# V in two places and other positions for the three steps from values to tokens, in a kernel of deformable convolution and spectral filters on one core

## The reference

```
x = x + silu(batchnorm(deform_conv2d(ln_c(x), offset(x), mask(x), weight)))   # 3x3 taps, bilinear gather of 4 corners per tap
t = tokens(x)                                            # (4, 1024, 64)
t = t + stu(ln_t(t))
# stu: U_plus, U_minus = causal convolutions of u with 16 filters phi (and with signs alternated)
#      out = sum_k s_k U_plus[k] @ Mpp[k] + sum_k s_k U_minus[k] @ Mpm[k] + 3 lags of u @ Mu
#      four branches (whole, half, quarter, eighth of the tokens), mixed by hard/soft weights
x = from_tokens(t)
```

## Time and profile before

| | us |
|---|---|
| median of 3 runs | 757.35 |
| lowest and highest of them | 754.41, 762.09 |
| the profiled execution | 751.24 |
| its span in the trace | 749.4 |

### The profile page before, as it was taken

One profiled execution on the slowest core, in us unless ns is written; L12 is line 12 of the kernel. 1 busy time (PEld: TensorE's weight loads), 2 busy tenths in 40 slices (PEclk: granted clock), 3 DMA queues, 4 the chain that ended last, 5 costly groups with the idle time before them and its releaser, 6 DMA issues.

```text
span 749.4 us, 13126 instructions
## 1 busy us (share of the span) xinstructions
PE 506.5 (68%) x5598; PEld 376.8 (50%) x5598; DVE 314.9 (42%) x800; ACT 179.7 (24%) x421; POOL 292.7 (39%) x295
## 2 busy tenths in 40 slices
PE   5976429246208845785889549891168648999998
PEld 3443105135106613564678329771156327788997
DVE  6467411868602703850438007187009025753000
ACT  1121012113004302321232102240033113334322
POOL 1257750634770372556253732237702745000000
PEclk9966558659557966986999759996569759899999
DMA  8526373811330131222121320113300321000000
GB/s 166 127 79 158 101 204 117 282 56 50 98 105 2 46 107 45 66 71 85 44 64 37 100 64 23 44 44 98 98 21 30 105 64 56 16 2 3 9 2 9
DMA packets 43778, 54.27 MB, mean 72 GB/s; under 512 B 24664, under 2 KB 34142, under 8 KB 43721
## 3 DMA queue, kind: packets, MB, share of 16 engines
q0 software_dynamic: 13824, 37.77, 17.1%
q1 hardware_dynamic: 23841, 13.42, 6.9%
q10 hardware_dynamic: 6056, 2.26, 1.3%
HBM read 50.12 MB, written 3.30 MB: 71 GB/s over the span
## 4 chain that ended last, share of the span: by engine, by line
PE 55%; another core or an unknown queue 25%; issue 10%; DVE 5%; ACT 4%; DMA 1%; SPq 0%; ACTq 0%; DVEq 0%
PE bank L888 30%; PE bank L900 7%; PE bank L760 2%; PE bank L834 2%; PE bank L824 2%; ACT u_conv L661 2%; PE bank L793 2%; PE bank L741 1%; PE bank L795 1%; PE bank L732 1%; PE bank L845 1%; PE bank L919 1%; ACT vT L628 1%; DMA filt<-in_L_ffn_phi_dram 1%
## 5 line engine op out<-in xcount | busy, mean ns | idle before, releaser
L269 POOL DMA_INDIRECT G<-corner_table,idx x288 | 290.0, 1007 | 343.9 <-DVE idx L362 155.2
L888 PE MATMUL bank<-filt,u_hi 128*64 128x256 f16 x2560 | 255.3, 291 | 135.1 <-issue 85.6
L888 PEld LDWEIGHTS bank<-filt,u_hi 128*64 128x64 f16 x2560 | 152.8, 114 | 172.0 <-issue 112.0
L888 PE MATMUL bank<-filt,u_lo 128*64 128x256 f16 x1280 | 198.9, 291 | 15.1 <-issue 15.1
L661 ACT ACTIVATE u_conv<-bank,f_scale 128x256 f32<-128x256 f32 x256 | 118.6, 474 | 303.8 <-PE bank L888 153.6
L900 PE MATMUL bank<-u_conv,mixw 128*64 128x256 f32 (+1 forms) x640 | 94.2, 377 | 9.9 <-issue 9.2
L888 PEld LDWEIGHTS bank<-filt,u_lo 128*64 128x64 f16 x1280 | 84.3, 117 | 24.6 <-issue 22.4
L455 DVE TENSOR_TENSOR G<-G,bank 128x2304 f32<-128x2304 f32 x32 | 81.5, 2548 | 0.3
L467 DVE TENSOR_SCALAR expo<-expo 128x128 f32<-128x128 f32 x16 | 3.6, 227 | 183.1 <-ACT expo L638 172.1
L459 DVE TENSOR_TENSOR V<-G 128x576 f32<-128x576 f32 x32 | 24.3, 758 | 110.0 <-PE bank L825 73.4
L900 PEld LDWEIGHTS bank<-u_conv,mixw 128*64 128x64 f32 x640 | 47.9, 155 | 20.5 <-issue 18.9
(11 more groups left out here) (158 smaller groups left out, 387.3 us busy)
## 6 DMA issues: line engine op xcount, KB each, us to landing
filt<-filter_rows SPq DMA_DIRECT2D x16, 514.0 KB, 9.1
G<-corner_table,idx POOLq DMA_INDIRECT x288
corner_table<-n_uT SPq DMA_DIRECT2D x12, 128.0 KB, 2.9
mixw<-in_x_dram SPq DMA_DIRECT2D x2, 512.0 KB, 6.0
filt<-in_L_ffn_M_phi_plus_dram SPq DMA_DIRECT2D x8, 128.0 KB, 4.9
out_dram<-o_sb ACTq DMA_DIRECT2D x8, 128.0 KB
filt<-n_L_ffn_M_phi_minus_dram ACTq DMA_DIRECT2D x4, 128.0 KB, 4.0
corner_table<-n_uT ACTq DMA_DIRECT2D x4, 128.0 KB, 3.3
```

The lines of the kernel that those rows point to most:

```text
L269: pool.indirect_dma_start(G[:, k, tap, :], None, corners[bp], bass.IndirectOffsetOnAxis(ap=idx[:, q % 2, k, tap:tap + 1], axis=0)).then_in ...
L888: last = pe.matmul(conv_ps[b2][C * src:C * src + C, 0:2 * P].rearrange("c (p a) -> c p a", p=2), u[:, NJ * bp + j2, b2, src], h, start=(j2 ...
```

## The change

V gets a second place, one for each row of a quarter: the even row writes and reads V[:, 0], the odd row V[:, 1]. With that, the write of V for row r waits until row r - 2 has been turned, not row r - 1. To make room, w_diag (used before the passes) and u_conv (used in them) share one tile. And the hosted steps move: of the even row, turning the values from filter 3 to 2, the convolution stays at 4, turning back from 5 to 6; of the odd row, from 11, 12 and 13 to 9, 11 and 13. The programs of VectorE and GpSimd keep their order.

```
-HOSTED_AT = ((3, 4, 5), (11, 12, 13))
+HOSTED_AT = ((2, 4, 6), (9, 11, 13))
...
-        V = sb("V", [P, 2, TAPS * C])
+        V = sb("V", [P, 2, 2, TAPS * C])
...
-        w_diag = sb("w_diag", [P, BRANCHES, 3, P])
...
-        u_conv = sb("u_conv", [P, 2, 2, 2, P])
+        late_tiles = sb("late_tiles", [P, 1536])
+        u_conv = late_tiles[:, 0:1024].rearrange("s (k b p a) -> s k b p a", k=2, b=2, p=2)
+        w_diag = late_tiles[:].rearrange("s (r v d) -> s r v d", r=BRANCHES, v=3)
...
                 if b2 == 0:
-                    dve.wait_ge(val_turned, START + 2 * q + p)
-                dve.tensor_tensor(V[:, b2].rearrange("s (t c) -> s t c", c=C), G[:, k, :, 0:C], G[:, k, :, C:2 * C], ALU.add
+                    dve.wait_ge(val_turned, START + 2 * q + p - 1)
+                dve.tensor_tensor(V[:, p, b2].rearrange("s (t c) -> s t c", c=C), G[:, k, :, 0:C], G[:, k, :, C:2 * C], ALU.add
                                   ).then_inc(v_ready[b2], 1)
...
                     for m in range(4):
-                        pe.transpose(val_ps[b2][:, P * m:P * m + P], V[:, b2, P * m:P * m + P], ident)
-                    last = pe.transpose(tail_ps[0:C, P * b2:P * b2 + P], V[:, b2, 4 * P:4 * P + C], ident)
+                        pe.transpose(val_ps[b2][:, P * m:P * m + P], V[:, r % 2, b2, P * m:P * m + P], ident)
+                    last = pe.transpose(tail_ps[0:C, P * b2:P * b2 + P], V[:, r % 2, b2, 4 * P:4 * P + C], ident)
```

## The result

The changed kernel takes 784.96 us (median of 4, 780.67 to 787.78), the kernel before, run beside it, 755.88 (4 runs, 748.04 to 762.09): a ratio of 1.041, interval 1.034 to 1.048, about 29 to 31 us slower. The profiled execution took 784.31 us against 751.24, 33 us more. The forecast was 773 (758 to 788): the sign and the range hold, the size is half of what came.

A forecast was written before the change was run, and what follows sets the result against it. The time was taken as TensorE's work plus the tails of the runs of gathers. The terms 19.5 + 3.2 + 5 - 11 - 1 = +15.7 us took the median of 757.35 to 773, range 758 to 788.

The forecast's parts named there:

- Part 1: Turn at filter 6, odd row's values at 9: TensorE waits for VectorE's 11.6 us chain in five passes, +19.5 us.
- half is taken back by the nine gathers behind: Lower bound of 15 us on the filter 9 waits: following gathers' tail would absorb half of passes 1 and 5's.
- The clock: Lower granted clock after TensorE's 4.4 us waits in passes 2 and 6: 1.6 us each, +3.2 us.
- my bound of 8: Upper bound of the clock loss, us: all five filter 9 waits put TensorE's array back to half rate.
- Part 2: V once per row: no gain on VectorE, but pass 2's gathers join into one run of 27, +5 us.
- the +5 for the join: Cost in us of pass 2's gathers joining into 27, most matmuls of the former gap moving behind the run.
- Part 3: Runs of 36 gathers in passes 0 and 4 split into 27 + 9, freeing TensorE earlier: -4 and -7, sum -11.
- Part 4: Two filters between hosted steps remove TensorE's waits for the vT copies: -1 us.
- my outer bound: Largest gain allowed for removing TensorE's waits for the vT copies: -2.4 us.
- nothing splits: Rival: the gather runs of passes 0 and 4 stay whole, +30 us, 787; chance 0.18.
- late fetch: Rival: TensorE's slow stretches come from late instruction fetch, not gathers; joining or splitting is irrelevant, +22, 779; chance 0.1.
- the 3.79 us: Pass 2, before: the third set of gathers' wait for V, and V's for turn_values, splitting the run.

The follow-up runs named there:

- run 3: Kernel before with V in two places and only the even row's steps moved, to filters 2, 4, 6: 777.96 us, ratio 1.013.
- run 4: Kernel before with V in two places and only the odd row's steps moved, to filters 9, 11, 13: 787.11 us, ratio 1.028.
- run 6: The changed kernel, unedited, profiled on another chip beside the kernel before: 804.61 us against 770.51, ratio 1.045.
- run 2: Kernel before with only the hosted steps moved (2, 4, 6 and 9, 11, 13), V in one place: 810.02 us, ratio 1.056.
- run 5: The kernel before, unedited, profiled once more on another chip: 767.32 us in its profiled execution.
- run 1: Changed kernel with hosted steps put back at filters 3, 4, 5 and 11, 12, 13, V in two places: 772.55 us, ratio 1.0065 to before.
- run 8: Kernel before with a rest of GpSimd, two small waited-for memsets, after every third gather: 591.41 us, ratio 0.7705.

## Why the prediction was right, and where its sizes were off

**Part 1, TensorE waits for VectorE's chain: right, to a few tenths, in the five passes priced.** Passes 1, 2, 3, 5, 6 were put at 4.8, 4.4, 2.4, 3.5, 4.4 (sum 19.5) and measured 5.06, 4.37, 2.39, 3.90, 4.36 (sum 20.1). Runs 3 and 4 show the rule behind it, filters between exponential and values, at two more distances. Pass 5 scatters more on other chips (4.75 in run 6, 5.59 in run 2). The bound "half is taken back by the nine gathers behind" did not come true: the fourth set waits for the same V, so it moves along with the turn.

**The clock: right in size for pass 6, charged to too few waits.** Windows of the kernel after, TensorE alone, in pass 6, ahead of the turn, behind it, and the next stretch:
```profile
680.00:705.00 25.00, 20.78 (x315) 1.00 0.01 2
705.00:711.00 6.00, 5.86 (x55) 0.72 0.01 3
711.00:716.00 5.00, 5.00 (x90) 1.00 0.00 0
```
0.28 of 6 us are 1.7 us, 1.6 was charged. Waiting 1.95 us (run 4) left that pass at 1.00. In passes 2 and 3, all engines as in the earlier trace rows, the 5 us some 2 us behind the waits of 4.37 and of 2.39 us:
```profile
396.00:401.00 5.00, 5.00 (x65) 4.16 (x66) 2.54 (x3) 2.55 (x6) 4.09 (x4) 0.82 0.31 98
490.00:495.00 5.00, 5.00 (x84) 4.49 (x82) 2.93 (x3) 2.27 (x6) 4.09 (x4) 1.00 0.32 86
```
65 matmuls ran where 84 did. But passes 1 and 5, where I had charged nothing, paid too. The 5 us right behind their waits of 5.06 and 3.90 us, TensorE alone:
```profile
307.80:312.80 5.00, 4.95 (x36) 0.53 0.19 57
646.70:651.70 5.00, 4.93 (x40) 0.66 0.17 52
```
The changed kernel and runs 2 and 6 have 17 waits of 3.9 us and more at filter 9, and behind every one the same 5 us have 0.50 to 0.71, so mostly the 1.2 GHz level. Behind the shorter ones it goes either way: 1.00 behind 2.39 us in the changed kernel and 1.95 in pass 6 of run 4, but in pass 3 of run 6 (2.37 us) and pass 2 of run 4 (1.96 us):
```profile
502.10:507.10 5.00, 4.97 (x48) 0.66 0.19 56
...
397.70:402.70 5.00, 4.94 (x48) 0.66 0.18 56
```
In those 5 us the five waits that I had priced lost 7.4 us (2.35, 1.7, 0, 1.7, 1.65), not 3.2, just under my bound of 8. Passes 1 and 5 came out near their terms all the same, because their granted clock over the whole pass did not change (0.77 and 0.77, 0.74 and 0.75): before, pass 1 had its low stretch at its end instead (0.69 from 313.5 to 320.5). That their totals fit is in part luck.

**Pass 6 adds up, with one term that I had not seen.** 4.36 of waiting, 1.7 of clock, and 1.36 us in which TensorE stood at the start of the pass for u_lo of the odd row. The timeline after:
```profile
664.95 0.23 DVE L468 TENSOR_SCALAR expo<-expo 128x128 f32<-128x128 f32 x1 [13.63 <-ACT expo L639]
...
671.30 0.29 DVE L491 SCALAR_TENSOR_TENSOR u_lo<-u_tok,u_hi 128x128 f16<-128x128 f32 x1
```
The sum is 7.4, as measured. From the exponential (664.6) to u_lo are 6.9 us, and the pass ends 4.4 us behind that exponential. In run 5 it ends 9.1 us behind it, and there is no such wait: TensorE was still held by the nine gathers of pass 5. Windows of run 5, TensorE alone, beside and behind these nine:
```profile
647.00:653.00 6.00, 2.77 (x35) 0.96 0.34 102
653.00:661.00 8.00, 5.59 (x52) 0.60 0.09 29
```
So the last filters cover VectorE's chain only where a tail makes them long. Runs 1, 2, 4 and 6 have the 1.4 us too, run 1 without any step moved, run 3 has not: it goes with where the tail lies, and isn't the moved steps' alone.

**Part 2, the join in pass 2: right in what happened, not shown as its effect.** The waits for V at L459 are gone, and stand at L468, as foreseen. The waits list after (us in total, times, longest):
```profile
DVE expo L468 <- ACT expo L639: 294.0, 14, 43.6
```
That line was 172.1 before; the waits ahead of the write of V, 73.4 behind the turn of V and 35.6 behind "remote", have gone into it, and VectorE is not done sooner. The run of pass 2 is one piece of 27 (337.8 to 372.4) and the pass 14.4 us longer on the first chip. On the second the kernel before had it joined too, at 84.4 us, and the changed one took 92.3, +7.9. The difference between the chips, 6.5 us, is in line with the +5 for the join, but run 1, which has V twice and the run joined, is only 0.65% slower as a whole. So V twice is no sizable loss by itself; the join comes and goes. The term was put on the wrong cause: runs 2 and 5 join with V once. And its price is not shown: in pass 3, 18 + 9 and 27 took the same time (93.5 in run 5, 93.6 before).

**Part 3, the splits: the step that failed.** I had -4 in pass 0 and -7 in pass 4. The splits came as foreseen in both, but brought less, and laid open a wait that I had set to none. Eight profiled executions, with the run of gathers, the wait for V at the odd row's turn and the length of the pass, in us:

| kernel | pass 0: run | wait | length | pass 4: run | wait | length |
|---|---|---|---|---|---|---|
| before | 36 | 0 | 84.5 | 36 | 0 | 73.3 |
| run 5 (before) | 36 | 0 | 84.6 | 27 + 9 | 0 | 69.4 |
| run 1 | 36 | 0 | 86.4 | 36 | 0 | 74.0 |
| run 4 | 36 | 0 | 87.0 | 36 | 0 | 73.6 |
| run 3 | 27 + 9 | 2.8 | 85.5 | 27 + 9 | 3.0 | 72.6 |
| after | 27 + 9 | 6.6 | 89.0 | 27 + 9 | 0.6 | 68.9 |
| run 6 (after) | 27 + 9 | 6.7 | 90.9 | 27 + 9 | 6.5 | 77.8 |
| run 2 | 27 + 9 | 5.8 | 89.6 | 27 + 9 | 6.2 | 78.2 |

Length less wait is 82.4 to 84.3 in pass 0 when split, against 84.5 to 87.0 unsplit; in pass 4 it is 68.3 to 72.0 against 73.3 to 74.0. So, as an estimate from these differences, a split is worth about 2 us in pass 0 and 3.5 in pass 4, half of what I had put. The wait depends on where the exponential comes. In pass 0 it came not at 205 to 210 but at 215.40, only behind the run: by then TensorE was free, ran on to filter 9 and stood there 6.55 us for V. The text had set the waits of passes 0 and 4 to none, as TensorE would be in the tail of a run; once the run is split there is no tail. In pass 4 of the first chip the exponential slipped through 3.7 us before the run ended, TensorE was held until 563.2 while VectorE worked, and the wait was 0.58; that is the case I had foreseen, and it gained 4.4 us. On the second chip it came at 575.47, 4.2 us behind the run's end, the wait was 6.54 and the pass took 8.4 us longer, against a kernel before that was already split. The estimate for pass 4 was made against one profiled execution; the other one of that kernel has 27 + 9. In place of -11, the two passes gave +0.1 on the first chip and +14.7 on the second.

**Part 4**, -1 for vT: the list of waits has 3.0 us in 2 places after, for 5.4 in 7 before, so 2.4 less, my outer bound. What that gave the passes is too small to be seen.

**The sum.** The passes grew by 33.4 us, against +15.7. Of the 17.7 between them, 11.1 are part 3 (8.5 in pass 0, 2.6 in pass 4), 6.6 the passes 2, 3 and 6 above their terms (3.4, 1.8, 1.4), 1 the gain of part 4, which no pass shows by itself, and -1 passes 1 and 5. The 1.4 of pass 6 has its row; pass 2 has such a wait of 1.38 us for u_lo at its start too (331.23), which leaves 2.0 and 1.8 us in passes 2 and 3 by subtraction, not traced further. The rival "nothing splits" was nearest in time (787), but that is luck, as its mechanism is not what happened: both runs split, and the splits paid less than the waits that they laid open.

**The rival of the late fetch.** I had put 0.1 on the tails being no matter of gathers. Run 8 leaves TensorE's program as it was and only paces GpSimd's gathers, and the tails are gone, with 23% of the time. So they are the gathers' doing. By which way a run of gathers stops TensorE (its instructions arriving late, its completions held up, or another) no run here decides, since pacing would help in each case; that stays open. The trace of the kernel before does show that what waits for TensorE moves late. The last matmul of a turn of V in pass 2, then ScalarE's copy and VectorE's write of the next V, which wait for that turn:
```profile
337.47 0.27 PE L825 MATMUL bank<-ident_swap,V 128*64 128x128 f32 x1
...
349.96 0.59 ACT L628 COPY vT<-bank 128x512 f32<-128x512 f32 x1 [2.64 <-remote]
...
350.03 0.76 DVE L459 TENSOR_TENSOR V<-G 128x576 f32<-128x576 f32 x1 [21.13 <-remote]
```
Both begin 12 us behind it, so the 3.79 us that the prediction laid to turn_values were not its work. In run 8 ScalarE's longest "remote" wait at u_conv is 3.8 us, in the kernel before 12.9.

## What to carry to other kernels

When a consumer is moved nearer to its producer on an in-order engine, count the work that lies between them in the engine's own time and set it against the chain of the other engine, read from the trace; here that gave the waits to a few tenths of a us where no run of gathers split. A gain expected from a wait that one profiled execution shows is only as good as that execution: where a stretch can fall two ways, look at a second one before pricing it. And when an engine's "issue" or "remote" time clusters beside one kind of transfer, pace that transfer before rearranging anything: here 192 idle memsets took 23% off, while the reordering had moved 4%.

## What the runs showed of the hardware that was not expected

- A run of indirect gathers from GpSimd (one per 1.25 us at best, 1.34 as a mean) leaves TensorE alone for some 10 us and then nearly stops it. Three gathers and a rest, 1.65 us per gather, do not: 141 matmuls in 12 us in their midst.
- The passage is narrow: 1.47 us per gather gave 704.55 us (0.916 of the kernel before), 1.56 gave 596.16 (0.786), with rests of the same length behind three and behind two gathers. A rest of 3.45 us behind nine, 1.67 us per gather, gave 707.85. Less time given to the gathers' queue made the whole kernel faster by up to 23%.
- On two chips the kernel before took different ways through a pass (18 + 9 or 27 gathers in pass 2, 36 or 27 + 9 in pass 4), with 7.6 us between the two lengths of pass 2 (76.8 and 84.4).
- The granted clock fell to 0.50 to 0.71 over the 5 us behind each of 17 waits of 3.9 to 6.7 us at filter 9; behind waits of 1.95 to 3.0 us it was 1.00 in some and 0.66 in others, at nearly the same length (2.39 and 2.37 us).
